# Loading the 64 skip factors of a state-space layer: two strided broadcasts, or one row spread by two copies

## The reference, cut to what matters

```
x = x + 0.5 * ffn(layernorm(x), lut, gate_idx, up_idx, down_idx)      # w = lut[idx]
x = x + mamba2(layernorm(x), ...)
x = x + 0.5 * ffn(layernorm(x), lut, gate_idx, up_idx, down_idx)

# in mamba2, H = 64 heads of P = 64 channels
yh = (Y_diag + Y_off).reshape(b, l, H, P) + D_param[None, None, :, None] * x
```

## Time and profile before

| | |
|---|---|
| median of 3 runs | 1380.05 us (1375.35 to 1380.12) |
| profiled execution | 1379.78 us |
| its span, first to last instruction | 1378.1 us |
| mean granted TensorE clock | 0.985 |
| busy: PE / DVE / ACT / POOL | 95% / 86% / 73% / 62% |
| q1, the kernel's own DMAs | 101952 packets, 134.76 MB |
| q8, instruction | 73 packets, 1.20 MB |

### The profile page before, as it was taken

One profiled execution on the slowest core, in us unless ns is written; L12 is line 12 of the kernel. 1 busy time (PEld: TensorE's weight loads), 2 busy tenths in 40 slices (PEclk: granted clock), 3 DMA queues, 4 the chain that ended last, 5 costly groups with the idle time before them and its releaser, 6 DMA issues.

```text
span 1378.1 us, 26980 instructions
## 1 busy us (share of the span) xinstructions
PE 1306.7 (95%) x8896; PEld 1117.1 (81%) x8896; DVE 1187.1 (86%) x2649; ACT 1001.6 (73%) x2043; POOL 850.9 (62%) x920
## 2 busy tenths in 40 slices
PE   7499999799999999999999999999999999998998
PEld 7498887678888888888888888888888888876887
DVE  7475566889999999999999999999999999997542
ACT  1015565898898888889888988888898888882442
POOL 1004221167687879778876978787787879674332
PEclk9799999999999999999999999999999999998999
DMA  6121002253443544444544555455445545435000
GB/s 137 51 106 45 16 16 70 61 114 117 108 102 119 124 116 120 115 122 110 103 112 116 120 123 119 113 122 114 110 100 116 126 119 117 97 99 203 16 16 31
DMA packets 102090, 136.49 MB, mean 99 GB/s; under 512 B 27744, under 2 KB 49856, under 8 KB 101824
## 3 DMA queue, kind: packets, MB, share of 16 engines
q1 hardware_dynamic: 101952, 134.76, 38.8%
HBM read 124.76 MB, written 9.96 MB: 98 GB/s over the span
## 4 chain that ended last, share of the span: by engine, by line
PE 55%; DVE 26%; issue 12%; ACT 3%; POOL 2%; DMA 0%; DVEq 0%; SPq 0%; POOLq 0%; ACTq 0%
PE psum L38 13%; PE psum L40 12%; PE psum L39 12%; DVE xs L1258 6%; PE psum L1707 5%; PE psum L1696 4%; PE psum L1487 4%; DVE inner L1309 4%; PE psum L1684 3%; DVE M L1285 3%; DVE xend L1275 3%; DVE psum L1317 2%; DVE mixed L1339 2%; PE psum L1673 1%; DVE carry L1309 1%
## 5 line engine op out<-in xcount | busy, mean ns | idle before, releaser
L827 ACT ACTIVATE M<-cum_row,cum_table 128x128 f32<-128x128 f32 x1024 | 312.1, 390 | 0.0
L1258 DVE SCALAR_TENSOR_TENSOR xs<-psum,conv_w_sb,xs 128x509 f32<-128x509 f32 (+2 forms) x384 | 282.9, 737 | 0.4
L987 POOL TENSOR_TENSOR hid_lo<-hid,hid_hi 128x512 fp32r<-128x512 f32 x128 | 206.8, 1616 | 55.8 <-PE psum L40 49.7
L1033 POOL TENSOR_TENSOR hid<-hid,sg 128x512 f32<-128x512 f32 x128 | 165.9, 1296 | 76.9 <-DVE hid L1326 76.8
L1019 POOL TENSOR_TENSOR squares<-squares,sq 128x512 f32<-128x512 f32 x124 | 161.0, 1298 | 72.0 <-ACT sq L804 72.0
L1285 DVE TENSOR_TENSOR M<-M,CB 128x1024 f32<-128x1024 f32 x128 | 184.6, 1442 | 0.0
L1707 PE MATMUL psum<-M,xdt 128*64 128x128 f32 x2048 | 140.5, 279 | 19.2 <-DVE psum L1317 19.0
L1707 PEld LDWEIGHTS psum<-M,xdt 128*64 128x64 f32 x2048 | 110.5, 137 | 42.0 <-DVE M L1285 23.0
L1684 PE MATMUL psum<-xend,B_tok 128*128 128x128 f32 x1024 | 138.3, 278 | 5.0 <-DVE carry L1309 4.5
L841 ACT ACTIVATE xs<-psum,conv_b_sb,conv_w_sb 128x512 f32<-128x512 f32 x128 | 99.2, 775 | 57.3 <-PE psum L40 56.7
L835 ACT ACTIVATE M<-M 128x1024 f32<-128x1024 f32 x128 | 134.5, 1051 | 0.5
(11 more groups left out here) (196 smaller groups left out, 3388.5 us busy)
## 6 DMA issues: line engine op xcount, KB each, us to landing
cum_row<-cum_scratch SPq DMA_DIRECT2D x256, 256.0 KB, 4.4
e_row<-e_scratch SPq DMA_DIRECT2D x256, 128.0 KB, 3.3
xw_raw<-L_attn_in_proj_w_dram SPq DMA_DIRECT2D x32, 128.0 KB, 4.9
wo_raw<-L_attn_out_proj_w_dram SPq DMA_DIRECT2D x32, 128.0 KB, 4.5
gw_raw<-L_attn_in_proj_w_dram SPq DMA_DIRECT2D x16, 256.0 KB, 5.8
x_res<-_attn_hidden_states_dram SPq DMA_DIRECT2D x4, 512.0 KB, 7.1
x_scratch<-x_res SPq DMA_DIRECT2D x4, 512.0 KB, 2.6
x_res<-x_scratch SPq DMA_DIRECT2D x1, 2048.0 KB, 8.5
```

What stands on the lines that cost most here:

```text
L827: last = nc.scalar.activation(M[:, v % 3, h, c * CH:(c + 1) * CH], cum_row[:, v % 2, h, c * CH:(c + 1) * CH], ACT.Relu, bias=scalar_of(CUM ...
L987: nc.gpsimd.tensor_tensor(hid_lo[:], hid[:, v % 2, :], hid_hi[:, v % 2, :].bitcast(F32), ALU.subtract).then_inc(hid_lo_done, 1)
L1033: nc.gpsimd.tensor_tensor(hid[:, v % 2, :], hid[:, v % 2, :], sg[:, v % 8, :], ALU.mult).then_inc(hid_done, 1)
L1258: nc.vector.scalar_tensor_tensor(xs[:, v % 7, shift:], psum[:, X_BANK + v % 2, 0:TT - shift], tap_of(v, step), xs[:, v % 7, shift:], ALU.m ...
```

## The change

`d_param` is loaded as one row of 64 values for all 128 partitions into a new tile `d_rows` (like `a_exp`). In tick 6 of the first FFN VectorE waits for the load and makes `d_sb` with two copies of 64 partitions x 32 values, from the even columns for the upper half and from the odd ones for the lower half. `chan_in` ends at 64, not at 80; VectorE's wait before the loop is for the two copies (`d_done`, its own semaphore, 2).

```diff
+    d_rows = sb("d_rows", [P, H], F32)
...
-    folded = sem("folded")
+    folded, d_done = sem("folded"), sem("d_done")
...
                 sp.dma_start(norm_sb[:], norm_w.rearrange("(k p) -> p k", p=P)).then_inc(chan_in, 16)
-                d_pairs = d_param.rearrange("(k two) -> two k", two=2)
-                for half in range(2):
-                    sp.dma_start(d_sb[half * HP:(half + 1) * HP, :], d_pairs[half].partition_broadcast(HP)).then_inc(chan_in, 16)
+            sp.dma_start(d_rows[:], d_param.partition_broadcast(P)).then_inc(chan_in, 16)
...
             def scale_wo(p):
                 act.wait_ge(wo_in[p % 2], (p // 2 + 1) * 16)
-                act.wait_ge(chan_in, 80)
+                act.wait_ge(chan_in, 64)
...
+            def spread_d():
+                dve.wait_ge(chan_in, 64)
+                heads = d_rows[:].rearrange("p (k two) -> p k two", two=2)
+                for half in range(2):
+                    rows = slice(half * HP, (half + 1) * HP)
+                    nc.vector.tensor_copy(d_sb[rows, :], heads[rows, :, half]).then_inc(d_done, 1)
...
+                if k == 6:
+                    spread_d()
...
-            dve.wait_ge(chan_in, 80)
+            dve.wait_ge(d_done, 2)
```

## The result

The changed kernel takes 1359.54 us (median of 4 runs, 1357.37 to 1360.62) against 1379.64 us before (4 runs): a ratio of 0.9862, 95% interval 0.9843 to 0.988, so 17 to 22 us less. The forecast was 1361.8 us, 18.3 us less; the interval holds that. The profiled execution took 1359.91 us, with a span of 1358.2 us.

A forecast was written before the change was run, and what follows sets the result against it. TensorE, busy 1306.7 of 1378.1 us, was taken as the bound, with a 16.59 us decode hole from late code. 1380.05 less 18.3 us (16.6 hole, 1.7 clock; other terms 0) gave 1361.8 us, range 1356 to 1369.

The forecast's parts named there:

- The hole is a late block of code, and the block waits behind the d_sb loads: TensorE's decode stop from 51.23 us: code due near 36 us was held by two d_sb loads until 65.8 us.
- -16.6 us for the hole: Decode transposes on TensorE: the code fetch served at 36 us removes the 16.59 us hole.
- -1.7 us for the clock: After the hole, 25 matmuls ran at 179 ns each against 112 ns at full clock; 25 x 67 ns saved.
- TensorE has two blocks of code at hand, not 2048 instructions: TensorE ran dry 505 instructions after its last fetch, near two fetches; by the 2048 rule, gain 0, chance 0.02.
- The row costs as a_exp does: The added row load, issued at 21.7 us, lands like a_exp (6.3 us), by about 28 to 32 us.
- The copies: 0: Two VectorE copies in tick 6, 0.4 us together, covered by 3.53 us of idle time; without cover 0.4.
- The gate spill beside the fetch: 0: Spill at 50.2 us beside the code block due then: 0, at worst a few us; rival about 1367 us, 0.07.
- no hole stayed: Rival: block held by SP's full queue or the fetch itself, so the decode hole stays, 1380 us; chance 0.04.
- nothing came back later: Rival: loads that now run early hit another block of the start-up, 1377 us or so; chance 0.02.
- the row was not served value by value: Rival: row load takes 76 us, code block comes 37 us later, 1417 us; chance 0.02.
- The difference is that all 64 partitions of a d_sb half read the same 32 addresses: Start-up loads: given as why 2048 d_sb values took 19.1 us while norm_sb's 4096 landed in 7.7 us.
- until they end: Code fetches stand behind the d_sb reads in the DMA engines; the fetch was served when the second load ended, 65.8 us.

The follow-up runs named there:

- e2_three_quarters: Changed kernel plus one and a half of the two old strided d_sb loads (3072 single values) into an unread tile; 1368.47 us, ratio 0.9932.
- e3_both: Changed kernel plus both old strided d_sb loads (4096 single values) into an unread tile; 1379.31 us, ratio 1.0005.
- e6_second_at_41: Kernel before, its second d_sb load moved behind gw_raw and a wait for the first normalised tile (41 us); 1361.38 us, ratio 0.988.
- e4_double: Changed kernel plus four such strided loads (8192 single values of the same 64 addresses) into an unread tile; 1386.3 us, ratio 1.0058.
- e1_half: Changed kernel plus one of the two old strided d_sb loads (2048 single values) into an unread tile; 1360.01 us, ratio 0.9866.
- e8_far_apart: Changed kernel plus two loads of the d_sb form, read from norm_w with the 32 addresses 512 B apart; 1359.99 us, ratio 0.9866.

## Why the prediction was right

**The hole is a late block of code, and the block waits behind the d_sb loads.** Right, and now shown by cause: the same kernel has a hole of 0, 7.55 and 16.86 us with 2048, 3072 and 4096 such values put back, and the fetch goes by at the end of the reads each time.

**-16.6 us for the hole, -1.7 us for the clock.** 18.4 us at the end of the decode, 18.3 forecast. The clock term does not grow with the hole: the 233 matmuls behind it took 28.09 us in the kernel before, 28.84 in e2_three_quarters (hole 7.55 us) and 27.80 in e3_both (16.86 us), against 26.2 us at the changed kernel's pace, so 1.9, 2.6 and 1.6 us. Behind the 2.26 us of e6_second_at_41 it was 0. The medians show 1.7 us more gain than these 18.4 us (1379.64 - 1359.54 = 20.1); that lies within the interval, and no trace ties it to the change. In the same way e3_both is 10.8 us slower than e2_three_quarters by the medians, with 9.3 us more hole.

**TensorE has two blocks of code at hand, not 2048 instructions.** The 2048 instructions of the Trainium skill (Runtime: NRT & Kernel Launch, Instruction fetch mechanics) would have let e3_both and e4_double run without a hole; they have holes of 16.86 and 18.72 us. In e4_double the second stop comes 127 matmuls after the restart, 254 instructions with their weight loads, one fetch's worth of 16 KB. The traces decide: TensorE gets through about two blocks, the one in use and one ahead.

**The row costs as a_exp does.** 6.4 us to landing, against 6.3. **The copies: 0.** 0.37 us in 3.53 us of idle time, forecast 0.4. **The gate spill beside the fetch: 0.** The number is right, but the meeting that was feared did not take place: the fetch went by before 49.5 us, the spill was issued at 50.25. In e1_half the two did meet, the fetch came at about 54 us, and TensorE still did not stop. Of the rivals none came: no hole stayed, nothing came back later, and the row was not served value by value.

**What was wrong though it cost nothing.** Two sentences of the working. "The difference is that all 64 partitions of a d_sb half read the same 32 addresses": e8_far_apart keeps that and is fast. And that fetches stand behind these reads "until they end": e4_double forecast on it was 29 us off. It is the reads handed over before the request that count, as e6_second_at_41 bears out. In the kernel before, both loads had been handed over by 29 us and the request came at about 35, so the two readings give the same number, and the forecast could not tell them apart. That the wrong one did no harm was luck. The upper bound of 76 us for the row was made from the first of these readings.

What stays open: which of the DMA engines or rings a fetch passes, and why reads within 256 B go at one per 9.4 ns, by the piece or by the step. The runs show the times, not the place. The order at the request is inferred from when the fetches went by; the moment of a request is not in the trace. How long a hole may be before the clock falls is open too: it stayed at 1.00 behind 2.26 us (e6_second_at_41) and was 0.69 behind 2.75 us (e4_double, where it had been low up to about 72 us as well, after the long hole).

## What to carry to other kernels

When TensorE stops in the middle of a loop with nothing to wait for, look at the instruction queue: a fetch that is missing for two blocks' worth of instructions was the sign here that code stood behind data, though the DMA engines looked only 5% busy. Small tables that every partition needs should be loaded as whole rows and spread on chip; if single values must be read, spread their addresses (64 B apart was enough here), or see to it that the reads handed over before a request end before the stock of code does. In this decode that is some 14 us after the request: TensorE stops 16.7 us after it (34.5 to 51.2 us) and needs the fetch 2.3 us before. A load of 19 us by itself, issued 9 us before the request, cost nothing. And a load that nobody needs for 200 us is not free for that reason: ask what is queued behind it.

## What the runs showed of the hardware that was not expected

Reads of 4 B from one piece of 256 B go through at one per 9.4 ns, all queued loads taken together; with 16 B between addresses, over 512 B, it is one per 4.8 ns, with 64 B or 512 B apart 4096 of them land in 4 to 6 us. A fetch goes through between two queued loads (e4_double, at 66 and 85 us), so doubling the harmful reads from 38 to 76 us cost 7.9 us and not 38. And half of them cost nothing: 19 us of reads shorten TensorE's stock of code without emptying it (e1_half), though with less than 1 us to spare.
